# Three GpSimd instructions of a graph-network kernel moved or replaced: a cast, a diagonal select, a running sum

## The chip, the cores and the metric

The kernel runs on one core of one Trainium2 chip. The metric is device time in microseconds (us), the median over runs: 674.09 us before the change (three runs, 673.4 to 678.29). The core has five engines with queues of their own, which meet through semaphores: TensorE (PE, with its weight loads as PEld), VectorE (DVE), ScalarE (ACT), GpSimd (POOL) and SyncE (SP, which here only issues loads).

## What is computed

64 graphs of 128 nodes with 64 features pass through four layers, each followed by a residual sum and a layer norm. The adjacency is symmetric, sparse, and has a 1 on every place of its diagonal (every node has its own loop); the node mask is all ones.

```python
x = _layernorm(x + _L0_gnn_ref(x, adj, ...))            # mean, max, min, std over neighbours
x = _layernorm(x + _L1_gnn_ref(x, adj, weight, bias))   # adj @ (x W) + b
x = _layernorm(x + _L2_gnn_ref(x, adj, nodemask, ...))  # weighted quantiles over a thinned neighbourhood
x = _layernorm(x + _L3_gnn_ref(x, adj))                 # (adj + I) x / row sum
# in L2, the thinning:
adj_ = jnp.where(eye[None], 1.0, adj)                   # every node its own neighbour
nb = (adj_ > 0) & (~eye)[None]
m = nb.sum(-1)
skip = jnp.where(m > 10, (m + 1) // 2, 1)
do_dil = (skip > 1) & mask
removed = nb & do_dil[..., None] & ((rank + 1) % skip[..., None] == 0)
```

## The kernel before

The 64 graphs go in eight turns of eight graphs (`G = 8`, `NG = 8`); `t` is a turn. Work is cut into named steps, and each engine has a hand-written order string (`TENSOR_ORDER`, `SCALAR_ORDER`, `VECTOR_ORDER`, `GPSIMD_ORDER`). An entry `name@lag` means that round `n` issues that step for turn `n + lag`; so one round holds the front of turn n, the middle of turn n-1 and the end of turn n-2. The engines' queues run in order, and a step begins with waits on semaphores. Nothing is scheduled at run time.

What the turn does, with the step names used below:

- `P` (DVE, L1304) makes a permutation matrix per graph, nodes sorted by degree. `Pb` (POOL, step `pb`, L1066) is its bf16 copy, used by the TensorE steps `sm` and `va`. TensorE `yr` (relab<-P,R) and `ap` (relab<-Cc,P) permute the adjacency; ScalarE evicts them in `ysb` (Cc<-relab, L753) and `adj` (adjP, L758).
- `mp` (DVE) makes `maskP`, the permuted 0/1 mask. TensorE `p1` ranks it. Then `se` (POOL, L1070, an affine select over 128x1024 bf16) sets its diagonal to 1 in place, under the name `selfT`. TensorE `va` adds the removed neighbours to it; ScalarE `vt` takes the result as `validT`, from which `p2`, `cr` and ScalarE `sg` make `sgnT`, the signs "has row n more than k neighbours".
- `sk` (POOL, nine instructions over 128x2) works out the skip numbers.
- Layer 0 picks neighbours by one-hot columns (`h0`, TensorE `g0`, evicted by ScalarE `e0` into slot0) and folds them by `tr:0` and `tr:1` (DVE, L1399 and L1413). TensorE `yl:0`/`yl:1` follow, ScalarE scales in `ys:0`/`ys:1` (wv<-pna, L850), DVE adds in `zf:0`/`zf:1` (L1430, L1431). `yl:1` waits for `zf:0`.
- Layer 2 does the same with `h2`, `g2`, `e2` (L908), sorts with a network of 66 min/max instructions (`so`, DVE L1474), weighs (`wr` on TensorE, `wg` on DVE L1487) and sums (`ag`, DVE L1497 and L1501). TensorE `c2:0`/`c2:1` (rest<-x2T,weights) wait for `ag`; between them stands ScalarE's `c2e:0` (hT).
- `n3x` (DVE, L1440) makes the last norm `xo`; `sc` (POOL, L1099) scatters it to HBM in eight indirect DMAs.
- `ov` (POOL, L1092) adds `sgnT` of the turn to a running sum `ovs`. After the last turn `check_counts` (DVE) waits for all of these and tests whether any row had more neighbours than the slots allow; if so, a general path would run (with these inputs it does not).
- `pre` steps are done once, in the first rounds: constants, weights, tables (`tables`, DVE L1208 to L1247; pcol is L1217), and on POOL `split_rows`, five instructions over 128x384 (L1056 to L1060) that split the row factors of turns 2 to 7 in three bf16 parts.

Of the kernel before, what the change touches and what calls it, by code (L numbers as in the profile page):

```python
# [54 lines left out]
KEEP = 4  # L55
# [78 lines left out]
class Turn:  # L134
# [23 lines left out]
    ys:0@0 ysb@1 ys:1@0"""  # L158
# [12 lines left out]
def adj_kernel(nc, x_nat, adj_rows, adj_cols, node_mask, wpack, wrows, out):  # L171

    with ExitStack() as ctx:
# [573 lines left out]
        def scalar_steps(act):  # L747
# [41 lines left out]
            def sg(t):  # L789
# [3 lines left out]
                before(act, "ovs", t, KEEP)  # L793
# [179 lines left out]
            return dict(ysb=ysb, adj=adj, kn=kn, k1=k1, dtc=dtc, vt=vt, k2=k2, sg=sg, xs=xs, qo=qo, pm=pm, pl=pl, rp=rp_, up=up_, ys=ys_, y2e=y2e, z3e=z3e, xr=xr_, xm=xm, xl=xl, ac=ac,  # L973
# [18 lines left out]
        def gpsimd_steps(pool):  # L992
# [123 lines left out]
        def vector_steps(dve):  # L1116
# [86 lines left out]
            def tables():  # L1203
# [28 lines left out]
                for at, to in runs(CAP0):  # L1232
                    V.memset(room0[:, at:to], float(CAP0[at]))
                for at, to in runs(CAP2):
                    V.memset(room2[:, 1 + at:1 + to], float(CAP2[at]))
                V.memset(room2[:, 0:1], 128.0)
                own(V.memset(room2[:, STEPS2 - 1:STEPS2], 0.0))
                V.tensor_tensor(room2[:, :], room2[:, :], step_is[:, :], ALU.mult)
# [515 lines left out]
```

## Time and profile before

| | |
|---|---|
| time, median of 3 runs | 674.09 us |
| span of the profiled execution | 669.3 us |
| PE busy | 491.7 us, 73% |
| DVE busy | 535.6 us, 80% |
| ACT busy | 364.5 us, 54% |
| POOL busy | 144.2 us, 22%, in 211 instructions |
| mean granted TensorE clock | 0.857 of full speed |

The profiled execution's span is 4.8 us under the median. "Busy" counts an instruction from start to end, so it includes the time in which an instruction has started and cannot go on. A row of the timeline reads: start in us, duration in us, engine, line, operation, output<-inputs, shapes, how many merged instructions, and in brackets the idle time before it and what ended that.

### The profile page before, as it was taken

The numbers are of one execution on the slowest core, as the hardware profiler recorded it, in microseconds if no ns is written. First come the engines' busy times: TensorE is split into PE (matmuls) and PEld (weight loads), VectorE is DVE, ScalarE is ACT, GpSimd is POOL, SyncE is SP. The second block draws the span as 40 slices with busy tenths as digits, with TensorE's granted clock in tenths as the row PEclk, the third lists the DMA queues.
The fourth block names the chain that finished last, engine by engine and source line by source line (L and its number), as shares of the span: only waits on it lengthen the run. The fifth ranks groups of instructions, "written<-read, shape, count | busy, mean of one in ns | idle before, by whom it ended". The sixth has DMA issues, their size and how long they took to land.

```text
span 669.3 us, 10465 instructions
## 1 busy us (share of the span) xinstructions
PE 491.7 (73%) x3380; PEld 326.3 (49%) x3419; DVE 535.6 (80%) x1514; ACT 364.5 (54%) x982; POOL 144.2 (22%) x211
## 2 busy tenths in 40 slices
PE   2466968957987889787979898879877986871420
PEld 2432655545655655474547555745564544540220
DVE  4995648998699988999899879997999699469221
ACT  0264577517773678457845685478548852350130
POOL 4500010042004400350035002500251062007023
PEclk9876998979799979999998799889989897555555
DMA  8300020002000200020002000200000000000000
GB/s 315 140 0 0 1 79 1 2 0 80 1 1 11 85 0 1 8 89 1 1 6 90 1 1 6 87 6 1 2 16 1 1 12 5 1 0 16 0 6 14
DMA packets 6573, 18.27 MB, mean 27 GB/s; under 512 B 1648, under 2 KB 1776, under 8 KB 6000
## 3 DMA queue, kind: packets, MB, share of 16 engines
q1 hardware_dynamic: 4464, 15.44, 6.6%
q0 software_dynamic: 2048, 2.10, 1.0%
q8 instruction: 28, 0.46, 0.3%
q14 instruction: 33, 0.27, 0.1%
HBM read 15.44 MB, written 2.10 MB: 26 GB/s over the span
## 4 chain that ended last, share of the span: by engine, by line
DVE 41%; issue 26%; PE 19%; POOL 6%; ACT 6%; POOLq 0%; DVEq 0%; ACTq 0%
DVE hot L1474 8%; DVE slot L1474 8%; DVE slot L1399 6%; PE pna L439 5%; POOL out_dram L1099 4%; PE ring L436 4%; PE pna L436 3%; PE relab L436 2%; PE rest L439 2%; PE rest L436 2%; DVE hot L1487 1%; DVE deg L1143 1%; PE ring L646 1%; DVE hot L1497 1%; DVE slot L1497 1%
## 5 line engine op out<-in xcount | busy, mean ns | idle before, releaser
L436 PE MATMUL ring<-hot,parts 128*64 128x384 bf16 (+3 forms) x753 | 137.9, 361 | 0.9
L1099 POOL DMA_INDIRECT out_dram<-xo,idx x64 | 76.4, 1193 | 130.5 <-DVE xo L1440 112.5
L899 ACT ACTIVATE slot<-ring 128x512 f32<-128x512 f32 (+1 forms) x128 | 61.7, 525 | 38.2 <-PE ring L436 33.9
L850 ACT ACTIVATE wv<-pna,rowP 128x64 f32<-128x64 f32 x128 | 28.0, 330 | 92.6 <-PE pna L436 92.6
L436 PEld LDWEIGHTS ring<-hot,parts 128*128 128x128 bf16 (+1 forms) x768 | 55.6, 108 | 39.9 <-issue 4.3
L1066 POOL CAST Pb<-P 128x1024 bf16<-128x1024 f32 x8 | 8.3, 1038 | 299.6 <-DVE P L1304 299.4
L1399 DVE TENSOR_TENSOR slot<-slot 128x128 f32<-128x128 f32 (+2 forms) x144 | 62.1, 484 | 2.7 <-ACT slot L899 0.7
L439 PE MATMUL ring<-emp,rowsel 112*128 112x512 bf16 (+1 forms) x128 | 45.3, 354 | 13.4 <-ACT slot L899 7.7
L1474 DVE TENSOR_TENSOR hot<-slot 128x64 f32<-128x64 f32 (+5 forms) x136 | 48.8, 392 | 3.8 <-ACT slot L908 3.7
L1474 DVE TENSOR_TENSOR slot<-slot 128x64 f32<-128x64 f32 (+5 forms) x136 | 51.1, 405 | 0.0
L439 PE MATMUL pna<-bdx,xT 128*128 128x384 f32 x64 | 31.5, 579 | 26.5 <-DVE zF L1431 26.5
L439 PE MATMUL rest<-x2T,weights 128*128 128x512 f32 x32 | 24.3, 851 | 23.6 <-DVE x2T L1501 15.9
L908 ACT ACTIVATE slot<-ring 128x384 f32<-128x384 f32 x64 | 31.4, 503 | 16.8 <-PE ring L436 16.4
L436 PE MATMUL pna<-weights,QQ 128*128 128x192 f32 x128 | 37.4, 378 | 0.0
L436 PE MATMUL pna<-wmm,slot 128*128 128x192 f32 x128 | 34.6, 355 | 0.0
L1474 DVE TENSOR_TENSOR hot<-hot 128x128 f32<-128x128 f32 (+3 forms) x96 | 33.4, 375 | 0.0
L1435 DVE TENSOR_REDUCE stB<-sqB 128x8 f32<-128x512 f32 x16 | 10.9, 682 | 26.6 <-ACT sqB L913 26.6
L826 ACT ACTIVATE zB<-rest,rowP 128x64 f32<-128x64 f32 x128 | 28.0, 340 | 6.9 <-PE rest L436 4.0
L1474 DVE TENSOR_TENSOR slot<-hot 128x64 f32<-128x64 f32 (+5 forms) x88 | 31.3, 378 | 0.0
L439 PE MATMUL ring<-sgnT,delta 32*128 32x512 bf16 (+2 forms) x48 | 14.9, 366 | 21.8 <-DVE slot L1487 20.1
L439 PEld LDWEIGHTS ring<-emp,rowsel 112*128 112x128 bf16 x128 | 12.8, 100 | 36.1 <-ACT slot L899 22.9
L439 PE MATMUL pna<-QQ,adjP 128*128 128x128 f32 x128 | 25.4, 379 | 4.8 <-ACT parts L822 4.7
(288 smaller groups left out, 1183.9 us busy)
## 6 DMA issues: line engine op xcount, KB each, us to landing
Cc<-adj_cols_dram SPq DMA_DIRECT2D x8, 512.0 KB, 3.9
R<-adj_rows_dram SPq DMA_DIRECT2D x8, 512.0 KB, 5.4
slot<-adj_rows_dram SPq DMA_DIRECT2D x4, 1024.0 KB, 12.1
xn<-x_nat_dram SPq DMA_DIRECT2D x8, 256.0 KB, 5.5
out_dram<-xo,idx POOLq DMA_INDIRECT x64, 2.3
weights<-wpack_dram SPq DMA_DIRECT2D x1, 608.5 KB, 8.1
biasr<-wrows_dram SPq DMA_DIRECT2D x1, 128.0 KB, 9.0
mask<-node_mask_dram SPq DMA_DIRECT2D x1, 8.0 KB, 4.7
```

The lines of the kernel that those rows point to most:

```text
L436: return mm(*a, start=False, stop=True, skip_group_check=True, **k)
L439: return mm(*a, start=True, stop=True, skip_group_check=True, **k)
L826: last = A(dst[:, g, :], src(g), ACT.Copy, scale=rowP[t.n % ROWKEEP][:, g, which:which + 1])
L850: last = A(ys[:, g, f, :], PQ[:, 256 * g + D * (f + 1):256 * g + D * (f + 2)], ACT.Copy, scale=rowP[t.n % ROWKEEP][:, 4 * h + g, AMP + f:A ...
L899: A(slot0[:, g, lo:hi], PG[ring["g0", t.n, 2 * g + j][0]][:, 0:hi - lo], ACT.Copy).then_inc(s["slot0"], 1)
L908: A(slot2[:, c, lo:hi], PG[ring["g2", t.n, 2 * c + j][0]][:, 0:hi - lo], ACT.Copy).then_inc(s["slot2"], 1)
L1066: V.tensor_copy(flat(Pb[:, :, :]), flat(P[:, :, :])).then_inc(s["Pb"], 1)
L1099: nc.gpsimd.indirect_dma_start(out=out, out_offset=bass.IndirectOffsetOnAxis(ap=idx[t.n % ROWKEEP][:, g:g + 1], axis=0), in_=xo[:, g, :], ...
L1399: return V.tensor_tensor(dst, dst, src, ALU.max)
L1435: V.tensor_reduce(st[:, 0, :], sq[:, :, :], AX.X, ALU.add).then_inc(s[signal], 1)
L1474: mark(("sort", k), V.tensor_tensor(low if is_min else wire(b, 1 - sb_, width), low, high, ALU.min if is_min else ALU.max))
L1497: mark(what, V.tensor_tensor(at, at, ranked(b), ALU.add))
```

## The change

Four things. The cast `pb` leaves POOL and becomes a ScalarE copy, placed between `ys:0` and `ysb`. The select `se` is no longer run in the normal path: `maskP` already has the diagonal when every node has its own loop, so `va` takes it as it is. `ov` and the four wide instructions behind it in `check_counts` go; the room test is left to the layer 0 count alone, whose slots are no wider. To know that the loops are there, a new load brings the diagonals (`own_loop`, 128x64) and a new DVE step `unusual` tests them and the node mask, once, in four instructions.

```diff
-    ys:0@0 ysb@1 ys:1@0"""
+    ys:0@0 pb@1 ysb@1 ys:1@0"""
 ...
     cm@1 so:0-20@-1 z3@-2 so:20-24@-1 n3d@-2 so:24-28@-1 n3x@-2
+    pre:6@-2"""
 GPSIMD_ORDER = """
-    pre:2@0 pre:0@2 sk@0 se@0 pre:1@1 pb@1 sc@-2 ov@-2 pre:3@-1"""
+    pre:2@0 pre:0@2 sk@0 pre:1@1 sc@-2 pre:3@-1"""
 ...
+            sp.dma_start(own_loop[:, :], adj_diag).then_inc(loops_in, 16)
 ...
             def va(t):
                 pe.wait_ge(s["dts"], t.dil())
-                pe.wait_ge(s["selfT"], given(t))
+                if t.fast:
+                    pe.wait_ge(s["maskP"], given(t))
 ...
+            def pb(t):
+                act.wait_ge(s["P"], given(t))
+                before(act, "va_ps", t)
+                A(flat(Pb[:, :, :]), flat(P[:, :, :]), ACT.Copy).then_inc(s["Pb"], 1)
 ...
-            def pb(t):
-                pool.wait_ge(s["P"], given(t))
-                before(pool, "va_ps", t)
-                V.tensor_copy(flat(Pb[:, :, :]), flat(P[:, :, :])).then_inc(s["Pb"], 1)
 ...
-            def ov(t):
-                pool.wait_ge(s["sgnT"], given(t))
-                V.tensor_tensor(flat(ovs[:, :, :]), flat(ovs[:, :, :]), flat(sgnT[t.n % KEEP][:, :, :]),
-                                ALU.add).then_inc(s["ovs"], 1)
 ...
+            def unusual():
+                dve.wait_ge(mask_in, 16)
+                dve.wait_ge(loops_in, 16)
+                dve.wait_ge(rows_in, 2)
+                own(V.tensor_scalar(rtmp[:, 0, :], own_loop[:, :], 0.0, None, ALU.is_le))
+                own(V.tensor_scalar(rtmp[:, 1, :], mask8[:, :], 0.5, None, ALU.is_lt))
+                own(V.tensor_tensor(rtmp[:, 0, :], rtmp[:, 0, :], rtmp[:, 1, :], ALU.max))
+                own(V.tensor_reduce(excess[:, 4:5], rtmp[:, 0, :], AX.X, ALU.max))
 ...
             def check_counts():
-                dve.wait_ge(s["ovs"], NG)
-                dve.wait_ge(s["xo"], NG)
-                own(V.tensor_scalar(tmp, ovs[:, :, :], 0.5 - NG, None, ALU.is_gt))
-                own(V.tensor_scalar(beyond, place[0:32, :], cap2[:, 0:1], None, ALU.is_ge))
-                own(V.tensor_tensor(tmp, tmp, beyond.unsqueeze(1).broadcast_to([32, PAIRS, N]), ALU.mult))
-                own(V.tensor_reduce(excess[0:32, 1:2], tmp.rearrange("p c n -> p (c n)"), AX.X, ALU.max))
-                V.tensor_tensor(excess[:, 3:4], excess[:, 0:1], excess[:, 1:2], ALU.max).then_inc(over_a, 1)
+                V.tensor_tensor(excess[:, 3:4], excess[:, 0:1], excess[:, 4:5], ALU.max).then_inc(over_a, 1)
```

The one-time tables lose the 32-row half of their capacity test (five memsets, a product and a reduction on DVE, one memset on POOL).

GpSimd's queue, around the second and third rounds. Before, the select, the cast for the next turn and the five `split_rows` instructions stand behind one another (L1086 is the last of the nine `sk` instructions):

```order
L1086 TENSOR_TENSOR skp<-skp 128x2
L1070 AFFINE_SELECT maskP<-maskP 128x1024
L1066 CAST Pb<-P 128x1024
L1056 CAST rowsb<-rows 128x48x8
L1057 TENSOR_TENSOR xo<-rows,rowsb 128x48x8
L1058 CAST rowsb<-xo 128x48x8
L1059 TENSOR_TENSOR xo<-xo,rowsb 128x48x8
L1060 CAST rowsb<-xo 128x48x8
L1078 TENSOR_SCALAR skp<-dcol 128x2
```

The same place in the changed kernel (its lines are numbered some 12 higher):

```order
L1093 TENSOR_TENSOR skp<-skp 128x2
L1068 CAST rowsb<-rows 128x48x8
L1069 TENSOR_TENSOR xo<-rows,rowsb 128x48x8
L1070 CAST rowsb<-xo 128x48x8
L1071 TENSOR_TENSOR xo<-xo,rowsb 128x48x8
L1072 CAST rowsb<-xo 128x48x8
L1085 TENSOR_SCALAR skp<-dcol 128x2
```

The five split instructions no longer stand behind the cast, which waits for the next turn's P; they follow `sk` and wait for the row factors alone.

ScalarE's queue, where round n-1 ends its layer 0 scaling (`ys:0` and `ys:1`). Before:

```order
L899 ACTIVATE slot<-ring 128x328
L850 ACTIVATE wv<-pna,rowP 128x64 x8
L753 ACTIVATE Cc<-relab 128x1024
L850 ACTIVATE wv<-pna,rowP 128x64 x8
L758 ACTIVATE adjP<-relab 128x1024
```

In the changed kernel:

```order
L912 ACTIVATE slot<-ring 128x328
L863 ACTIVATE wv<-pna,rowP 128x64 x8
L772 ACTIVATE Pb<-P 128x1024
L762 ACTIVATE Cc<-relab 128x1024
L863 ACTIVATE wv<-pna,rowP 128x64 x8
L767 ACTIVATE adjP<-relab 128x1024
```

The cast stands ahead of the eviction `ysb`, so `ysb` waits for it too. The same holds at the program's start, where the cast of turn 0 is the third instruction of the queue and `ysb` of turn 0 the fourth.

## Rows read from the trace of the kernel before

**Rows 1.** Timeline of POOL, the cast Pb in three rounds (start, duration, ...)

```profile
276.80 1.04 POOL L1066 CAST Pb<-P 128x1024 bf16<-128x1024 f32 x1 [44.92 <-DVE P L1304]
343.77 1.04 POOL L1066 CAST Pb<-P 128x1024 bf16<-128x1024 f32 x1 [43.04 <-DVE P L1304]
412.96 1.04 POOL L1066 CAST Pb<-P 128x1024 bf16<-128x1024 f32 x1 [45.26 <-DVE P L1304]
```

**Rows 2.** Chain that ended last, one round: start, us, what

```profile
343.70 2.78 DVE slot L1399 x6
...
356.87 1.11 DVE slot L1474
...
366.67 1.12 DVE hot L1497
```

**Rows 3.** POOL's groups by line and shape: busy us, mean ns | idle before

```profile
L1092 POOL TENSOR_TENSOR ovs<-ovs,sgnT 32x512 bf16<-32x512 bf16 x8 | 11.9, 1486 | 0.2
L1070 POOL TENSOR_SCALAR_AFFINE_SELECT maskP<-maskP 128x1024 bf16<-128x1024 bf16 x8 | 10.6, 1325 | 12.8 <-PE relab L439 12.8
L1066 POOL CAST Pb<-P 128x1024 bf16<-128x1024 f32 x8 | 8.3, 1038 | 299.6 <-DVE P L1304 299.4 <-POOL rowsb L1060 0.2
```

**Rows 4.** Timeline of DVE: the same instructions with and without POOL beside them

```profile
151.47 0.22 DVE L1474 TENSOR_TENSOR slot<-slot,hot 128x64 f32<-128x64 f32 x1
...
336.23 2.47 DVE L1399 TENSOR_TENSOR slot<-slot 128x128 f32<-128x128 f32 x7
...
343.62 3.31 DVE L1399 TENSOR_TENSOR slot<-slot 128x128 f32<-128x128 f32 x7
...
356.79 1.17 DVE L1474 TENSOR_TENSOR slot<-slot,hot 128x64 f32<-128x64 f32 x1
...
567.59 0.22 DVE L1497 TENSOR_TENSOR hot<-hot,slot 128x64 f32<-128x64 f32 x1
```

**Rows 5.** Timeline of ACT and DVE around ysb, ys:1 and zf:1 of one round

```profile
212.00 1.02 ACT L753 ACTIVATE Cc<-relab 128x1024 f32<-128x1024 f32 x1 [0.76 <-PE relab L439]
221.20 1.75 ACT L850 ACTIVATE wv<-pna,rowP 128x64 f32<-128x64 f32 x8 [8.17 <-PE pna L436]
223.37 0.42 DVE L1430 TENSOR_TENSOR zF<-pna,wv 128x256 f32<-128x256 f32 x1
```

**Rows 6.** Timeline of DVE around the five split_rows instructions

```profile
116.91 0.22 DVE L1474 TENSOR_TENSOR hot<-slot 128x64 f32<-128x64 f32 x1 [1.32 <-ACT slot L908]
...
134.60 5.58 DVE L1399 TENSOR_TENSOR slot<-slot 128x128 f32<-128x128 f32 x7
```

**Rows 7.** A ScalarE group, SBUF to SBUF; one small DVE instruction in a chain of its kind

```profile
L966 ACT ACTIVATE parts<-rest_ 128x512 bf16<-128x512 f32 x8 | 5.0, 631 | 4.1 <-DVE rest_ L1526 4.1
...
112.16 0.19 DVE L1149 TENSOR_SCALAR rows<-rows 128x48 f32<-128x48 f32 x1
```

**Rows 8.** The start: a piece of the chain that ended last

```profile
16.61 0.92 ACT Cc L753
```

**Rows 9.** The end: timeline, and the landing of the scatters (last number, us)

```profile
656.75 0.96 POOL L1099 DMA_INDIRECT out_dram<-xo,idx  x1 [0.30 <-issue]
658.99 0.41 DVE L1631 TENSOR_SCALAR zB<-ovs 32x512 f32<-32x512 bf16 x1 [11.13 <-POOL ovs L1092]
...
662.10 0.14 DVE L1638 CAST overi<-over 1x1 int32<-1x1 f32 x1
...
out_dram<-xo,idx POOLq DMA_INDIRECT x64, 2.3
```

**Rows 10.** Timeline of PE: matmuls behind waits, in two rounds

```profile
305.54 1.10 PE L439 MATMUL rest<-x2T,weights 128*128 128x512 f32 x2 [0.98 <-ACT hT L971]
...
350.95 0.88 PE L439 MATMUL pna<-bdx,xT 128*128 128x384 f32 x2 [3.16 <-DVE zF L1431]
...
370.41 1.13 PE L439 MATMUL rest<-x2T,weights 128*128 128x512 f32 x2 [1.83 <-DVE x2T L1501]
...
372.51 2.05 PE L439 MATMUL rest<-x2T,weights 128*128 128x512 f32 x2 [0.98 <-ACT hT L971]
```

More of the change, by code:

```diff
@@ L41 @@
 W0, W2 = sum(CAP0), sum(CAP2)
+assert CAP2 == CAP0[:K2] and K0 == K2 + 2 and DILATE_ABOVE == K2 - 1
 SPLIT0, SPLIT2 = OFF0[4], OFF2[3]
@@ L163, with adj_kernel @@
     h2:6-8@-1 h0:3-4@0 h2:8-11@-1 h0:4-9@0 me@0 ng@0 we@0 z2@-2 n2d@-2 h0:9-13@0 n2x@-2 pre:5@-1 em@0 pre:4@0
-    cm@1 so:0-20@-1 z3@-2 so:20-24@-1 n3d@-2 so:24-28@-1 n3x@-2"""
+    cm@1 so:0-20@-1 z3@-2 so:20-24@-1 n3d@-2 so:24-28@-1 n3x@-2
+    pre:6@-2"""
 GPSIMD_ORDER = """
-    pre:2@0 pre:0@2 sk@0 se@0 pre:1@1 pb@1 sc@-2 ov@-2 pre:3@-1"""
+    pre:2@0 pre:0@2 sk@0 pre:1@1 sc@-2 pre:3@-1"""
 SYNC_ORDER = """
     lc@-1 lr@-1 lx@-1"""
-def adj_kernel(nc, x_nat, adj_rows, adj_cols, node_mask, wpack, wrows, out):
+def adj_kernel(nc, x_nat, adj_rows, adj_cols, adj_diag, node_mask, wpack, wrows, out):
     with ExitStack() as ctx:
@@ L330, in adj_kernel @@
         mask_in = sem("mask_in")
+        loops_in = sem("loops_in")
         bias_in = sem("bias_in")
@@ L347, in given, with late @@
             return t.n * per + (per if k is None else k)
+        def late(t, per=1, k=None):
+            return t.g * per + (per if k is None else k)
         def before(eng, name, t, back=1, per=1, k=None):
@@ L511, in va @@
                 pe.wait_ge(s["dts"], t.dil())
-                pe.wait_ge(s["selfT"], given(t))
+                if t.fast:
+                    pe.wait_ge(s["maskP"], given(t))
+                else:
+                    pe.wait_ge(s["selfT"], late(t))
                 for h in range(2):
@@ L792, in sg @@
                 before(act, "g2_ps", t, KEEP, 2 * PAIRS)
-                before(act, "ovs", t, KEEP)
                 if not t.fast:
@@ L971, in c2e @@
                 A(hT[:, a, :, :].rearrange("p c n -> p (c n)"), PZ[:, 512:1024], ACT.Relu, bias=b1t).then_inc(s["hT"], 1)
-            return dict(ysb=ysb, adj=adj, kn=kn, k1=k1, dtc=dtc, vt=vt, k2=k2, sg=sg, xs=xs, qo=qo, pm=pm, pl=pl, rp=rp_, up=up_, ys=ys_, y2e=y2e, z3e=z3e, xr=xr_, xm=xm, xl=xl, ac=ac,
+            return dict(ysb=ysb, pb=pb, adj=adj, kn=kn, k1=k1, dtc=dtc, vt=vt, k2=k2, sg=sg, xs=xs, qo=qo, pm=pm, pl=pl, rp=rp_, up=up_, ys=ys_, y2e=y2e, z3e=z3e, xr=xr_, xm=xm, xl=xl, ac=ac,
                         sd=sd, mts=mts, e0=e0, e2=e2, n0q=n0q, n0r=n0r, n1q=n1q, n1r=n1r, n2q=n2q, n2r=n2r, n3q=n3q,
@@ L1232, in tables @@
                 for at, to in runs(CAP0):
[L1233 to L1238, printed above, removed]
+                    mark("own", V.memset(room0[:, at:to], float(CAP0[at])))
+                need("own")
                 own(V.tensor_tensor(room0[:, :], room0[:, :], slot_is[:, :], ALU.mult))
                 V.tensor_reduce(cap0[:, :], room0[:, :], AX.X, ALU.add)
-                V.tensor_reduce(cap2[:, :], room2[:, :], AX.X, ALU.add)
                 step2 = step_is[:, 1:1 + K2].unsqueeze(2).broadcast_to([32, K2, D])
@@ L1638, in check_counts @@
                 V.tensor_copy(overi[0:1, :], over[0:1, :]).then_inc(over_c, 1)
-            once = (prepare, weigh_in, tables, rank_weights, lambda: degrees(OTHERS), lambda: factors(OTHERS, 2))
+            once = (prepare, weigh_in, tables, rank_weights, lambda: degrees(OTHERS), lambda: factors(OTHERS, 2),
+                    unusual)
             def pre(t, k):
@@ L1666, in adj_kernel @@
                 b1 b2 b3 general2 c2:0 c2:1 c3 c6""",
-            "scalar": """ysb adj kn:0 k1 dtc:0 kn:1 dtc:1 kn:2 dtc:2 kn:3 dtc:3 vt k2 sg xs qo pm pl rp up ac sd mts
+            "scalar": """pb ysb adj kn:0 k1 dtc:0 kn:1 dtc:1 kn:2 dtc:2 kn:3 dtc:3 vt k2 sg xs qo pm pl rp up ac sd mts
                 ys:0 ys:1 n0q n0r b1e n1q n1r b3e xh xm xl c2e:0 c2e:1 y2e n2q n2r xr z3e n3q n3r""",
-            "gpsimd": "pb sk:0 se sk:1 sk:2 sk:3 sc",
+            "gpsimd": "sk:0 se sk:1 sk:2 sk:3 sc",
             "vector": """cm gt P nb:0 mp rw dr:0 nb:1 dr:1 nb:2 dr:2 nb:3 dr:3 ng me we general0 zf:0 zf:1
```

16 lines of the change are left out of this document (5 added, 11 removed).

## The prediction

> **What bounds the kernel now.** The page comes first: DVE is the busiest engine (80%), PE next (73%), and POOL is busy for 22% only, so GpSimd is not short of time. What matters is whom it stops. The chain that ended last, read for one round, answers that. A round is what lies between two casts Pb: 343.77 - 276.80 = 66.97 us, and 412.96 - 343.77 = 69.19 us [rows 1]. In each the chain runs on DVE through the sort, the folds and the weighing to the sum `ag`, then over PE's and ACT's steps from `c2:0` to the last `g2`, and back to DVE's sort. In DVE's part stand three pieces that are longer than their neighbours: the folds at 343.70, one sort instruction at 356.87 and one instruction of `ag` at 366.67 [rows 2].
>
> The timeline of DVE says why. The same seven folds take 2.47 us in `tr:0` and 3.31 us in `tr:1`, which runs while POOL casts Pb at 343.77 [rows 1, 4]: 0.84 us lost. A sort instruction over 128x64 takes 0.22 us in the round that has no `ov`, and 1.17 us in the round that has one [rows 4]: 0.95 us lost. An instruction of `ag` takes 0.22 us where no `se` runs [rows 4] and 1.12 us where one does [rows 2]: 0.90 us lost. Together 2.69 us of a round of 67 to 69 us, all of them on the chain; POOL's three instructions last 1.04, 1.49 and 1.33 us on average [rows 3].
>
> A rule of the Trainium skill speaks to this: "SBUF — State Buffer" says that VectorE and GpSimd share a pair of SBUF ports under an exclusive lock, held for a whole instruction, and that a VectorE instruction with two SBUF inputs contends with a GpSimd instruction that reads SBUF. Read strictly, the rule would have DVE lose each POOL instruction's whole length, an estimate of 3.9 us a round by their means, and the three removals together could give 6 x 1.04 + 6 x 1.33 + 7 x 1.49 = 24.7 us. The trace agrees on who is stopped, but shows 2.69 us a round, 17.1 us over the same counts; the sum goes by the rows.
>
> **The change part by part.** Rounds with a cast and a sort in full swing: casts of turns 2 to 7, six of them (in turn 1, near 74 us, DVE waits for ACT anyway, and I count nothing). Selects of turns 2 to 7, six; that of turn 1 falls into a wait of DVE.
>
> *Cast off POOL:* 6 x 0.84 = 5.0 us. On ACT the copy of 128x1024 has no row. From below it costs 0.63 us, the 128x512 copy between SBUF tiles, from above twice that, 1.26 [rows 7]; I take 1.05. It is hidden: before `ysb` ACT idles 0.76 us, so `ysb` slips by 0.3 (by 0.5 at the upper bound), and behind it ACT idles another 8.17 us before `ys:1` [rows 5]. What waits for `ysb` (`ap` on PE, `nb` on DVE) is queued behind `yl:1` and `zf:1`, some 9 us later; what waits for `Pb` (`sm`) is later still. Without that cover it would cost 1.05 a round.
>
> *Select removed:* 6 x 0.90 = 5.4 us. It lies just ahead of `c2:0`, which waits for `ag`, and nothing else holds `c2:0`.
>
> *Running sum removed:* seven lie in the rounds or the drain, each 0.95 on DVE. But the next meeting point is `zf:1`: `ys:1` ends at 221.20 + 1.75 = 222.95 and `zf:1` starts at 223.37 [rows 5], so DVE had 0.42 us to spare over ACT. DVE, freed of 0.95, arrives early and waits. I count 7 x 0.4 = 2.8; between 0 and 6.6.
>
> *split_rows moves:* beside it and the cast the folds took 5.58 instead of 2.47 us [rows 4, 6]. Its five instructions now start as soon as DVE has made the row factors, which is just ahead of a place where DVE waits 1.32 us for ACT and then sorts [rows 6]. Only what falls into the wait is free: between 0 and 1.3, I take 0.7.
>
> *Start:* DVE carries nearly all of the chain there too. The select of turn 0 ran beside the table pcol; I take 0.9, as in the rounds. The cast of turn 0 no longer stalls DVE (0.8), but on ACT it pushes `ysb` of turn 0, which is on the chain [rows 8], back by about 1.0. The tables' dropped small instructions give 0.3, of which little passes, since ACT's results are due soon after. Net 0.9, between -0.3 and 2.
>
> *unusual:* four chained instructions on DVE in the round that ends turn 0, at 0.19 us [rows 7] and a hand-over each: costs 0.9 us, on the chain. Its inputs have been there for long. The load behind it, 32 KB once, stands last in SP's first batch, and the loads of turn 1 queued behind it wait for turn 0's data to be used anyway: 0.
>
> *Scatters:* no longer behind the cast, they start some 10 us earlier in a round, beside `tr:0`. A scatter is not on the chain, and `n3x` waits for the one before for a whole round. 0.
>
> *End:* the last scatter is issued at 656.75 and lands about 2.3 us later, at 659.05. Now the test's last instruction ends at 662.10 + 0.14 = 662.24, because it waits for `ov`, which stands behind eight scatters (11.13 us of waiting) [rows 9]. After the change the test is done long before, and the landing sets the end: 3.2 us.
>
> Sum: 5.0 + 5.4 + 2.8 + 0.7 + 0.9 - 0.9 + 3.2 = 17.1 us.
>
> *The clock.* PE's granted clock falls to the lower level (1.2 of 2.4 GHz) at two places of a round. Behind its wait of 3.16 us for `zf:0` [rows 10] it fell in all five rounds from 208 us on. Around `c2:1` it fell in some rounds only: the same two matmuls take 2.05 us in one and 1.10 in the other [rows 10], and the round with the fall is 69.19 - 66.97 = 2.2 us longer [rows 1]. The granted clock by stretches shows such a fall in four of six rounds, at most 4 x 2.2 = 8.8 us in all. What PE did before it: little, with a wait of 1.83 us for `ag` in it [rows 10]. This wait shrinks by the select's 0.90, and the 3.16 by the cast's 0.84. So falls should get rarer, not more frequent. I take 3 us, a third of the 8.8; the bounds are -2 and +10 (the latter with the first place cured too, which lets `ov`'s other 0.55 a round through).
>
> Total 20.1 us. Against the profiled execution's span: 669.3 - 20.1 = 649.2 us. That span lies 4.8 under the median, and I carry that over: 674.1 - 20.1 = **654.0 us**.
>
> **The rivals.**
> - *Half of it is absorbed.* DVE's freed time turns into waits for ACT and PE, as shown for `ov`. For it: PE is busy 73%, and `zf:1` has 0.42 us of slack only. Against it: the cast's and the select's losses stand directly ahead of `zf:0` and `c2:0`, for which PE waits 3.16 and 1.83 us. With `ov` at 0, the clock as before and the cast or the select at half: 17.1 - 2.8 - 2.7 = 11.6, so 662; down to 8 us, 666. Chance 0.22.
> - *The clock stays up.* 17.1 + 8 to 10 us: 647 to 649. For it: the round that kept it at `c2:1` had the same waits, so it was close already. Against it: 2.3 us of idling before `yl:1` remain. Chance 0.15.
> - *The stalls stay.* DVE's long instructions come from something else that stays, the scatters say, or ScalarE's copy now stops DVE. Then only the end's 3.2 us and little more come: 670, within 1%. Against it: the stalls sit on different lines and go with POOL's instruction each time, and ACT copies between SBUF tiles all along. Chance 0.04.
> - *Slower.* The copy on ACT is slow or waits late, and `ys:1` slips. It decides from where the copy passes the cover: 0.76 + 8.17 = 8.9 us. To end over 1% slower it must lose 17 + 6.7 us in seven rounds, 3.4 each beyond the cover: a copy of 12.3 us, ten times the upper bound. Chance 0.02.
> - The forecast itself, a gain of 15 to 24 us, 650 to 659: 0.57.
>
> **How the numbers follow.** The predicted time is the forecast's. The range takes the forecast, nearly all of the clock case, and the better half of the absorbed case: 646 to 662. About 1% of the time, 6.7 us, is what a measurement can tell from no change. Faster by more: 0.57 + 0.15 + 0.21 of the absorbed case = 0.93; within 1%: 0.05; slower 0.02.
>
> **What would show it.** In the profile after: no L1399 group of seven above 2.5 us outside the split; the 128x64 instructions of the sort and of `ag` at 0.22 throughout; POOL busy down by some 30 us; ACT's Pb copy near 1.05 us, and idle behind it; a wait of about 0.5 us of DVE at `zf:1` for ACT; PE's wait before `yl:1` at 2.3 and before `c2:0` at 0.9; rounds of 64 to 66.5 us; the last DVE instruction ahead of the last scatter. Long folds beside a scatter would prove the stall theory wrong; short folds with rounds as long as before would prove the chain wrong.

## The result, and the profile after

The changed kernel takes 649.19 us (median of four runs, 646.34 to 652.76) against 673.75 us (median of four) for the kernel before in the same comparison: a ratio of 0.9676, 95% interval 0.9636 to 0.9716, or 24.6 us less. The forecast was 654.0, its range 646 to 662. The profiled execution took 646.34 us with a span of 644.8, that of before had 669.3: 24.5 us.

The head of the page after (spans in us):

```profile
span 644.8 us, 10421 instructions
...
PE 482.3 (75%) x3380; PEld 320.0 (50%) x3419; DVE 514.6 (80%) x1504; ACT 370.4 (57%) x990; POOL 112.8 (17%) x186
...
PEclk9866998999899989989998999899989997555555
```

POOL's busy time falls by 31.4 us, DVE's by 21.0. The mean granted clock is 0.874 against 0.857. The timeline of DVE, at the folds of one `tr:1` and at the `zf:1` of the next round, shows what [rows 1, 4] showed of before, now without POOL beside it, and a new wait:

```profile
266.76 2.46 DVE L1404 TENSOR_TENSOR slot<-slot 128x128 f32<-128x128 f32 x7
...
343.94 0.22 DVE L1479 TENSOR_TENSOR slot<-slot,hot 128x64 f32<-128x64 f32 x1
...
345.98 0.42 DVE L1435 TENSOR_TENSOR zF<-pna,wv 128x256 f32<-128x256 f32 x1 [0.49 <-ACT wv L863]
```

The seven folds take 2.46 us where they took 3.31, the 128x64 instruction of the sort 0.22 where it took 1.17, and DVE waits 0.49 us for ScalarE at `zf:1`, as forecast. ScalarE in the same round (timeline):

```profile
334.92 1.10 ACT L772 ACTIVATE Pb<-P 128x1024 bf16<-128x1024 f32 x1
335.86 1.07 ACT L762 ACTIVATE Cc<-relab 128x1024 f32<-128x1024 f32 x1
344.19 1.75 ACT L863 ACTIVATE wv<-pna,rowP 128x64 f32<-128x64 f32 x8 [7.26 <-PE pna L442]
```

The cast takes 1.10 us there (1.04 to 1.11 over the eight), `ysb` stands behind it, and 7.26 us of idling are left ahead of `ys:1` [rows 5: 8.17].

Rounds, cut at the start of P, first of before and then of after. Behind the length of a round stand the busy time (and number of instructions) of PE, PEld, DVE, ACT and POOL, then the granted clock, the DMA share and GB/s:

```profile
206.66:275.51 68.85, 58.31 (x424) 39.08 (x428) 61.82 (x171) 44.61 (x122) 15.31 (x20) 0.93 0.08 24
275.51:342.48 66.97, 55.81 (x424) 37.11 (x428) 61.73 (x172) 44.28 (x122) 15.32 (x20) 0.97 0.08 25
342.48:411.67 69.19, 58.65 (x424) 39.55 (x428) 61.83 (x171) 44.60 (x122) 15.31 (x20) 0.93 0.07 24
411.67:480.11 68.44, 57.40 (x424) 38.77 (x428) 61.81 (x172) 44.50 (x122) 15.33 (x20) 0.95 0.07 24
```

```profile
199.70:265.62 65.92, 56.01 (x424) 37.69 (x428) 59.15 (x172) 45.34 (x123) 10.46 (x17) 0.97 0.08 25
265.62:330.50 64.88, 55.87 (x424) 37.52 (x428) 59.17 (x171) 45.07 (x123) 11.91 (x18) 0.97 0.08 25
330.50:395.39 64.89, 55.89 (x424) 37.52 (x428) 59.17 (x171) 45.06 (x123) 11.92 (x18) 0.97 0.08 26
395.39:460.27 64.88, 55.89 (x424) 37.53 (x428) 59.17 (x171) 45.07 (x123) 11.91 (x18) 0.97 0.08 25
```

Two of these compare like with like: the rounds with the clock at 0.97 that fall only behind `zf:0`, 66.97 before and 64.88 after. They differ by 2.09 us. The sum had 0.84 + 0.90 + 0.4 = 2.14. The other three rounds of before are 1.5 to 2.2 us longer at a clock of 0.93 to 0.95; after the change one round is 1.0 longer, and none falls under 0.97.

Where the 24.5 us lie, by the same marks in both traces:

| stretch | before | after | won | in the sum |
|---|---|---|---|---|
| start to P of turn 1 | 72.95 | 70.17 | 2.78 | 0.9 |
| to P of turn 3 | 133.71 | 129.53 | 4.18 | 0.84 + 0.90 + 0.7 - 0.9 = 1.54 |
| to P of turn 7 (four rounds) | 273.45 | 260.57 | 12.88 | 4 x 2.14 = 8.56, and clock |
| to the last xo | 166.79 | 162.87 | 3.92 | 0.84 + 0.90 + 3 x 0.4 = 2.94 |
| last xo to the end | 22.4 | 21.6 | 0.8 | 3.2 |
| total | 669.3 | 644.8 | 24.5 | 17.1, and 3 for the clock |

### The profile page after: what moved, and what is told of

Read it like the earlier page. It is cut to its first block, busy times and chain, and to the rows that moved or that the text cites. A ratio compares the mean times of both kernels' runs of the same rounds, so it can differ in the third digit from the quotient of the medians.

```text
span 644.8 us, 10421 instructions
## 1 busy us (share of the span) xinstructions
PE 482.3 (75%) x3380; PEld 320.0 (50%) x3419; DVE 514.6 (80%) x1504; ACT 370.4 (57%) x990; POOL 112.8 (17%) x186
## 4 chain that ended last, share of the span: by engine, by line
DVE 34%; issue 27%; PE 22%; ACT 8%; POOL 6%; POOLq 0%; DVEq 0%; ACTq 0%
DVE hot L1479 7%; DVE slot L1479 7%; PE pna L445 6%; DVE slot L1404 5%; PE pna L442 5%; POOL out_dram L1099 5%; PE ring L442 4%; PE relab L442 2%; PE rest L442 2%; DVE deg L1143 1%; ACT wv L863 1%; PE ring L655 1%; DVE slot L1502 1%; DVE P L1309 1%; DVE hot L1492 1%
## 5 line engine op out<-in xcount | busy, mean ns | idle before, releaser
L1099 POOL DMA_INDIRECT out_dram<-xo,idx x64 | 78.1, 1220 | 309.9 <-DVE xo L1445 292.9
L1404 DVE TENSOR_TENSOR slot<-slot 128x128 f32<-128x128 f32 (+2 forms) x144 | 53.1, 424 | 2.8 <-ACT slot L912 0.9
L1479 DVE TENSOR_TENSOR hot<-slot 128x64 f32<-128x64 f32 (+5 forms) x136 | 50.8, 407 | 3.5 <-ACT slot L921 3.5
L445 PE MATMUL pna<-bdx,xT 128*128 128x384 f32 x64 | 28.6, 530 | 16.5 <-DVE zF L1436 16.5
L445 PE MATMUL rest<-x2T,weights 128*128 128x512 f32 x32 | 22.3, 785 | 18.1 <-DVE x2T L1506 10.4
L1085 POOL TENSOR_SCALAR skp<-dcol 128x2 f32<-128x2 f32 x8 | 2.1, 264 | 175.7 <-ACT dcol L780 175.7
L445 PE MATMUL ring<-sgnT,delta 32*128 32x512 bf16 (+2 forms) x48 | 14.6, 364 | 22.4 <-DVE slot L1492 20.3
L839 ACT ACTIVATE m<-pna,rowP 128x64 f32<-128x64 f32 x128 | 28.7, 394 | 0.1
```

The costliest lines, as they stand in the source:

```text
L445: return mm(*a, start=True, stop=True, skip_group_check=True, **k)
L839: last = A(dst[:, g, :], src(g), ACT.Copy, scale=rowP[t.n % ROWKEEP][:, g, which:which + 1])
L1099: nc.gpsimd.indirect_dma_start(out=out, out_offset=bass.IndirectOffsetOnAxis(ap=idx[t.n % ROWKEEP][:, g:g + 1], axis=0), in_=xo[:, g, :], ...
L1404: return V.tensor_tensor(dst, dst, src, ALU.max)
L1479: mark(("sort", k), V.tensor_tensor(low if is_min else wire(b, 1 - sb_, width), low, high, ALU.min if is_min else ALU.max))
```

## The experiments

### One part alone

Three kernels each take one part of the change to the kernel before.

```diff
 # the cast alone
-    ys:0@0 ysb@1 ys:1@0
+    ys:0@0 pb@1 ysb@1 ys:1@0
-    ... sk@0 se@0 pre:1@1 pb@1 sc@-2 ov@-2 ...
+    ... sk@0 se@0 pre:1@1 sc@-2 ov@-2 ...
```

> The kernel before with the cast alone moved to ScalarE. Stall theory: the seven folds beside the cast fall from 3.31 to 2.47 us in six rounds, 5.0 us, less 0.2 at the start (0.8 won on DVE, 1.0 lost on ysb of turn 0), plus 0.7 for the split: 5.5 us, 668 against 674. PE's wait for zf:0 falls from 3.16 to about 2.3, TensorE's clock falls behind it still. Absorbed theory: the 0.84 us turns into a wait for ACT at zf:1, so less than 2 us are won. Clock theory (the gain of the whole change is mostly fewer falls of the clock around c2:1): no gain of that kind here, since the wait for ag stays 1.83.

Measured: 666.18 us against 670.46, ratio 0.9949 (0.9917 to 0.9982), some 3.4 us. The profiled span was 663.6.

```diff
 # the select alone
-    ... sk@0 se@0 pre:1@1 ...
+    ... sk@0 pre:1@1 ...
+                if t.fast:
+                    pe.wait_ge(s["maskP"], given(t))
```

> The kernel before with the select alone left out, va waits for maskP. Stall theory: instructions of ag all at 0.22 us, 6 x 0.90 = 5.4, plus 0.9 at the start: 6.3 us. Clock theory: PE's wait for ag falls from 1.83 to 0.93, and with it the fall of the granted clock around c2:1 goes in most of the four rounds that show it, up to 8.8 us on top: 6 to 15 us, and the second c2 matmul pair takes 1.10 in each round. Absorbed theory: under 3 us.

Measured: four runs, 652.76, 664.87, 665.84 and 671.43 us, against 670.46. Their mean granted clocks were 0.892, 0.861, 0.854 and 0.844, in the same order: the same program, and 18.7 us between the runs. No ratio is given for them: by their median the select alone is worth 5.1 us, by the fastest run 17.7. The rounds say more. In the profiled execution one round (337.08 to 403.12) has a clock of 0.97 and its one fall behind `zf:0`, as the like round of before has; it takes 66.04 us against 66.97, which is 0.93 less where the sum had 0.90.

```diff
 # the running sum alone
-    ... sc@-2 ov@-2 ...
+    ... sc@-2 ...
-                own(V.tensor_scalar(tmp, ovs[:, :, :], 0.5 - NG, None, ALU.is_gt))
 ...
```

> The kernel before with the running sum and its test alone left out. As predicted: 0.4 us in each of seven rounds, 2.8, and 3.2 at the end: 6.0. As the changed kernel's trace suggests: the end gives 0.7 only, because something behind the last scatter holds the end 11.8 us from its issue, so 2.8 + 0.7 = 3.5 us, and DVE waits about 0.5 us for ScalarE at zf:1. With ov's 0.95 let through in full where the clock stays up: up to 6 us in the rounds.

Measured: 669.29 us, ratio 0.9997 (0.9967 to 1.0027): nothing.

The stalls first. The groups of DVE's 128x64 instructions in the sort and in `ag`, with mean ns behind the comma, first of the kernel with the sum alone removed:

```profile
L1473 DVE TENSOR_TENSOR slot<-slot,hot 128x64 f32<-128x64 f32 x40 | 8.6, 214 | 0.0
L1496 DVE TENSOR_TENSOR hot<-hot,slot 128x64 f32<-128x64 f32 x8 | 7.1, 888 | 0.0
```

and of the kernel with the select alone removed:

```profile
L1480 DVE TENSOR_TENSOR slot<-slot,hot 128x64 f32<-128x64 f32 x40 | 13.4, 334 | 0.0
L1503 DVE TENSOR_TENSOR hot<-hot,slot 128x64 f32<-128x64 f32 x8 | 1.7, 216 | 0.0
```

With the sum gone the sort is at 214 ns and `ag` still at 888; with the select gone `ag` is at 216 and the sort still at 334. So the sum's and the select's stalls were assigned rightly. DVE's busy time in the four rounds from P of turn 3 to P of turn 7 adds up too: a round has 0.73 us less without the cast, 0.95 less without the select and 0.88 less without the sum, 2.56 together, against 2.63 in the changed kernel.

But the times do not follow. With the cast alone gone, the seven folds of `tr:1` take 2.46 us in every round, and yet the four rounds (200.94 to 474.64) take 273.70 us, no less than before. The trace of that kernel shows why. GpSimd's queue no longer waits for P, so the scatters run earlier, and with them the running sum moves: it now stands beside the last two folds, ahead of `zf:0` (POOL and DVE):

```profile
273.50 1.39 POOL L1092 TENSOR_TENSOR ovs<-ovs,sgnT 32x512 bf16<-32x512 bf16 x1
```

```profile
273.80 1.91 DVE L1399 TENSOR_TENSOR slot<-slot 128x128 f32<-128x128 f32 x2
```

These two folds take 0.94 us in the kernel before:

```profile
347.45 0.94 DVE L1399 TENSOR_TENSOR slot<-slot 128x128 f32<-128x128 f32 x2
```

So ahead of `zf:0` DVE wins 0.85 us and loses 0.97, and PE's wait for `zf:0` goes from 3.16 to 3.28 us. What DVE wins behind `zf:0`, where the sum no longer stands, becomes a wait at `zf:1`:

```profile
355.95 0.42 DVE L1430 TENSOR_TENSOR zF<-pna,wv 128x256 f32<-128x256 f32 x1 [1.91 <-ACT wv L855]
```

That wait is for `ys:1`, behind a `yl:1` that ran wholly at the lower clock; in a round where the clock recovered sooner the wait is 0.30. "The cast alone" is therefore not the cast's stall alone: the kernel puts another stall in its place. The 5.7 us by which its profiled execution is shorter lie at the start (1.6) and in the two rounds where `split_rows` moved (4.1). In the full change this cannot happen, since the sum is gone as well.

With the sum alone gone, PE's second `c2` pair took 2.03 to 2.05 us in all six rounds from 167 us on, against 1.94 to 2.05 in three of six in the kernel before (the others 1.10), so what DVE gave back, the clock took.

### The cast put back, and two probes in its place

These start from the changed kernel.

```diff
-    ys:0@0 pb@1 ysb@1 ys:1@0
+    ys:0@0 ysb@1 ys:1@0
-    ... pre:1@1 sc@-2 ...
+    ... pre:1@1 pb@1 sc@-2 ...
```

> The changed kernel with the cast alone put back on GpSimd, in its old place between the split and the scatters. Stall theory: folds of tr:1 at 3.3 again in six rounds, 5.0 us slower than the changed kernel, and 0.8 at the start against 1.0 won on ysb; 654 to 655 against 649. If the wait for zf:0 grows back to about 3.2 and brings falls of the clock in the rounds that had none: up to 2 us more. Absorbed theory: DVE has 0.5 us to spare at zf:1 now, so only 0.35 of the 0.84 us a round is lost, 2 us.

Measured: 653.49 us, ratio 0.9745 (0.9701 to 0.9788), span 651.8: 4.3 us over the changed kernel by the medians. The folds of `tr:1` are back at 3.31 us. That is just under the expected 654 to 655.

The next two leave the real cast on ScalarE and give GpSimd something without use in its old place:

```diff
+            def pz(t):
+                pool.wait_ge(s["P"], given(t))
 ...
+                V.tensor_copy(scratch[:, 0:1024], flat(P[:, :, :]))   # e5
+                V.memset(scratch[:, 0:1200], 0.0)                     # e6, in its stead
 ...
-    ... pre:1@1 sc@-2 ...
+    ... pre:1@1 pz@1 sc@-2 ...
```

> The changed kernel plus one GpSimd cast a turn from P into a tile that nobody reads, in the old cast's place (128x1024 f32 to bf16, 1.04 us). Stall theory (GpSimd's port use stops the folds): the folds of tr:1 take 3.3 instead of 2.46 us in each round, some 5 us slower than the changed kernel: 650 to 655 of span, as in the run with the cast put back. Dependency theory (the old cast cost time because Pb came late or because of its semaphores): nothing waits for this one, so the folds stay at 2.46 and the time at the changed kernel's.

> The same with a memset of 128x1200 bf16, which writes SBUF for about as long (1.05 us by biasb's 1.81 us for 2048) and reads nothing. If what stops VectorE is GpSimd's reading, the folds stay at 2.46 and the span within 1 us of the changed kernel's with the same clock. If any use of SBUF by GpSimd stops it, the folds take 3.3 again and the run is like that with the cast.

Measured: with the read 656.17 us, ratio 0.969 (0.957 to 0.981), span 654.5; with the write 650.29, ratio 0.964 (0.955 to 0.973), span 649.4. The intervals overlap; the rows decide. Timelines of POOL and DVE, with the cast without use:

```profile
270.16 1.04 POOL L1080 CAST scratch<-P 128x1024 bf16<-128x1024 f32 x1 [46.02 <-DVE P L1317]
```

```profile
270.01 3.31 DVE L1412 TENSOR_TENSOR slot<-slot 128x128 f32<-128x128 f32 x7
```

and with the memset:

```profile
269.88 1.10 POOL L1080 MEMSET scratch<- 128x1200 bf16 x1 [45.18 <-DVE P L1317]
```

```profile
269.74 2.46 DVE L1412 TENSOR_TENSOR slot<-slot 128x128 f32<-128x128 f32 x7
```

A cast that nobody waits for costs the folds the same 0.85 us as the real one. A memset that is slightly longer and writes the same SBUF costs them nothing. So for the cast it is GpSimd's reading that stops VectorE, not a late Pb, a semaphore, or SBUF traffic as such. That is also what the Trainium skill, "SBUF — State Buffer" (Who interferes with whom), states: a VectorE instruction with two SBUF inputs contends with a GpSimd instruction that reads SBUF, not with one that only writes. The traces agree on that. The page says further (SBUF: two separate sides) that the one which starts first has the ports for its whole instruction and the other is blocked. The traces show a little less, 0.85 us lost of 1.04, and don't show where the rest is. The select and the sum were only removed, not replaced by such a pair of probes. GpSimd's scatters lie beside `tr:0` and `tr:1` in the changed kernel, and the folds take 2.47 and 2.46 us there, as without them.

Both probes also queue the second `split_rows` behind their instruction, as the kernel before did. With the memset, P of turn 1 to P of turn 3 takes 131.31 us (71.63 to 202.94), in the changed kernel 129.53 (70.17 to 199.70). PE's wait for `zf:0` in there is 6.08 us in place of 1.07. By this pair the split's new place is worth up to 1.8 us; other kernels with the split in its new place took 129.6 to 131.3, so the clock can take most of that again.

### Filling PE's wait

```diff
+            def fz(t):
 ...
+                pe.wait_ge(s["x2"], t.n)
 ...
+                for k in range(9):      # 12 in the kernel before
+                    new(bank(PZ, 0), identb[:, :], onesb[:, :])
-    ... yr@0 yl:1@-1
+    ... yr@0 fz@-1 yl:1@-1
```

> The changed kernel plus nine matmuls of 512 columns without use in PE's wait of 2.33 us for zf:0, seven times. Clock theory: the granted clock no longer falls behind this wait, yl:1 runs at 0.81 and 0.49 throughout, DVE's wait of 0.5 us at zf:1 goes, and a round takes 64.2 instead of 64.9 us in the four rounds that had the fall: 3 us faster, span 642. Rival: a round that kept its clock at the first place tends to lose it around c2:1 instead (as 199.7 to 265.6 in the changed kernel did, 65.8 to 65.9 us), so the fill moves the fall and the time stays or grows by up to 1 us a round. Slower by 0.2 a round if the nine do not fit into the wait.

> The kernel before plus twelve matmuls of 512 columns without use in PE's wait of 3.16 us for zf:0, seven times. It holds the clock at the first place in both kernels, so that what is left between this run and the filled changed kernel (span 642.0) is what the change itself takes off the chain. Stall theory: rounds of 66.5 us (64.3 of the filled changed kernel plus 0.84 + 0.90 + 0.4), span near 660, 18 us above the filled changed kernel. Clock theory (the change's gain is mostly clock): the span comes within 10 us of 642. If the fall around c2:1 stays, since its wait of 1.83 us for ag is untouched, rounds stay at 68 to 69 and the span at 665 to 669.

Measured on the changed kernel: 646.0 us, ratio 0.9588 (0.9501 to 0.9675), four spans from 642.0 to 644.6. The rounds of the profiled execution:

```profile
202.13:266.41 64.28, 56.88 (x438) 36.89 (x437) 59.02 (x171) 45.11 (x123) 10.46 (x17) 1.00 0.08 25
266.41:330.69 64.28, 56.88 (x438) 36.87 (x437) 59.03 (x171) 45.11 (x123) 11.88 (x18) 1.00 0.09 26
330.69:394.96 64.27, 56.88 (x438) 36.87 (x437) 59.02 (x172) 45.12 (x123) 11.89 (x18) 1.00 0.08 26
394.96:460.78 65.82, 58.44 (x438) 38.45 (x437) 59.11 (x171) 45.33 (x123) 11.88 (x18) 0.97 0.08 25
```

Three rounds keep the full clock, DVE's wait at `zf:1` is gone, and they take 64.28 us, 0.6 less than the 64.88 with a fall. This is the 0.5 us of `ov` that the forecast had only in its upper bound. In the kernel before the same kind of edit gives nothing: 670.17 us, ratio 0.9976 (0.9935 to 1.0018), though the mean clock of its ten runs was 0.859 to 0.875, against 0.844 to 0.863 without the fill. Two rounds of its profiled execution, which at 676.29 us is 6 us longer than the median:

```profile
205.57:275.58 70.01, 60.47 (x435) 39.40 (x440) 61.68 (x171) 44.65 (x122) 15.43 (x20) 0.93 0.07 24
275.58:346.92 71.34, 61.86 (x435) 40.62 (x440) 61.88 (x172) 44.84 (x122) 15.25 (x20) 0.90 0.07 23
```

The first two matmuls of `yl:1` took 0.88 us, as at full clock, in every round from 205 us on. The fall came a few microseconds later instead (PE's timeline; `xt` took 1.09 us in the kernel before at full clock):

```profile
284.05 0.88 PE L439 MATMUL pna<-bdx,xT 128*128 128x384 f32 x2 [0.57 <-DVE zF L1439]
...
293.31 1.97 PE L439 MATMUL pna<-P,xn 128*64 128x128 f32 x16 [0.36 <-DVE zF L1439]
...
306.06 1.82 PE L439 MATMUL rest<-x2T,weights 128*128 128x512 f32 x2 [2.40 <-DVE x2T L1509]
308.87 2.05 PE L439 MATMUL rest<-x2T,weights 128*128 128x512 f32 x2 [0.98 <-ACT hT L979]
```

So curing the clock at one place can move its fall to another, and in the kernel before it did. Filled kernel against filled kernel the change is worth 24.2 us by the medians (670.17 - 646.0). The stall theory expected 18 and the clock theory less than 10, and neither came out. Nearest came the third case of that expectation, that the fall around `c2:1` stays and the span is 665 to 669: the ten spans run from 666.1 to 675.8, with a median of 668.3, but the rounds of the profiled execution grew to as much as 71.3 us, which it did not foresee. What PE must have done for the clock to fall just there is left open.

### The end

```diff
 # behind the last turn's eight scatters (e8)
+                if t.n == NG - 1:
 ...
+                    own(V.tensor_tensor(flat(ovs[:, :, :]), flat(ovs[:, :, :]), flat(sgnT[t.n % KEEP][:, :, :]), ALU.add))
 # or in their stead, on SP (e10)
+            sp.wait_ge(s["xo"], NG)
+            sp.dma_start(last, xo[:, :, :]).then_inc(last_out, 16)
 ...
```

The second of these leaves out the last turn's scatters, so its last 1024 rows lie in sorted order and not in their places; it serves this question alone. Each has one run: 650.4 and 637.43 us.

> The changed kernel plus one GpSimd instruction behind the last scatter (the running sum's 32x512 addition, some 1.2 us when alone). In the changed kernel 11.83 us lie between the start of the last scatter and the end. If the end hangs on GpSimd's queue running dry, they grow by 1.2 to 13.0. If it hangs on the landing of the last scatter and its signal, they stay 11.8.

> The changed kernel, but the last turn's 1024 rows are stored by one plain load-queue transfer of SP in their sorted order, without its eight scatters; these rows are not put in their places. GpSimd's last instruction is then a scatter of the turn before. If the end hangs on GpSimd's queue running dry, nothing of GpSimd is late any more, and the end comes about 7 us behind the test's last instruction (625.08 + 0.14 + 7.06 = 632.3), or about 4 us (the median landing of such transfers) plus a few behind the last xo at 623.1: 631 to 634. If it hangs on a fixed time behind the last store of any kind, 623.2 + 11.8 = 635.

From the start of the last scatter to the end it is 12.6 us in the kernel before, 11.8 in the changed one, 11.4 with the sum alone removed, and 12.8 with the instruction put behind the scatters. That is the growth that the queue case of the expectation gives. The view of the line at which the program's engines meet for the last time shows what these are made of. `POOLq` is GpSimd's sequencer. Each engine runs a DRAIN there, and GpSimd's EVENT_SEMAPHORE, which comes behind the last of them, lets all go on to read the test's result. A row has durations in ns, then the start; start and duration give the end, so GpSimd's DRAIN ends at 647.7 + 16.5 = 664.2. Before:

```profile
L1656 POOLq EVENT_SEMAPHORE  x2: 17/17/17, 664.3 to 664.3; - x2
...
L1656 POOLq DRAIN  x1: 16490/16490/16490, 647.7 to 647.7; - x1
...
L1656 DVEq DRAIN  x1: 180/180/180, 662.1 to 662.1; - x1
```

After:

```profile
L1654 POOLq EVENT_SEMAPHORE  x2: 17/17/17, 639.3 to 639.4; - x2
...
L1654 POOLq DRAIN  x1: 15337/15337/15337, 623.9 to 623.9; - x1
...
L1654 SPq COMPARE_BRANCH  x1: 33/33/33, 635.1 to 635.1; - x1
```

And without the last scatters:

```profile
L1661 POOLq EVENT_SEMAPHORE  x2: 17/17/17, 630.5 to 630.6; - x2
L1661 POOLq DRAIN  x1: 17677/17677/17677, 584.2 to 584.2; - x1
...
L1661 DVEq DRAIN  x1: 178/178/178, 628.9 to 628.9; - x1
L1661 SPq COMPARE_BRANCH  x1: 33/33/33, 630.4 to 630.4; - x1
```

SP's COMPARE_BRANCH stands behind SP's wait for the scatters, so in the changed kernel they had all landed by 635.1, about as the forecast had it (2.2 us behind the start of the last). But GpSimd's DRAIN went on to 639.2, which is 5.3 us behind its last instruction (633.9). In the kernel before it is the same 5.3 us (658.9 to 664.2), and so it is, 5.29 to 5.33 us, in every kernel of this study in which the last turn is scattered (with the added instruction, from GpSimd's wait behind it). VectorE's DRAIN was over at 662.3 there, 1.9 us sooner. So the test did not set the end in the kernel before either; GpSimd did. Without the last scatters GpSimd is done at 601.9, and SP's wait for its plain store, until 630.3, comes last. The end, 635.8, is 6.8 us behind the test (629.0), as one case of the expectation had it, but it is the store that holds it. The other case, a fixed 11.8 us behind the last store's start, is out: the last `xo` came at 626.96 here, and the end would have been near 639.

Behind the meeting come 0.8 to 0.9 us in all kernels, and then one branch of PE, which is the last thing in the trace:

```profile
bacc.py:44 PEldq COMPARE_BRANCH  x1: 4238/4238/4238, 665.1 to 665.1; - x1
```

This is of the kernel before; it takes 4.66 us in the changed one, 4.2 to 4.7 in all kernels without filling matmuls and 3.3 to 3.6 in the four with them. Why it differs is open. The end's gain adds up from these rows: 1.2 us for the running sum ahead of the DRAIN, less 0.4 for that branch, 0.8. Against a plain store the last eight scatters cost 12.8 us: 21.6 us from the last `xo` to the end in the changed kernel, 8.8 without them (626.96 to 635.8).

### A better version

```diff
-    ys:0@0 pb@1 ysb@1 ys:1@0
+    ys:0@0 ysb@1 pb@1 ys:1@0
-    pre:6@-2"""
+"""
             def check_counts():
+                unusual()
 # and the nine filling matmuls ahead of yl:1
```

> The changed kernel with three edits: the nine filling matmuls, the cast of a turn behind ysb instead of ahead of it, and the loop and mask test at the end of the program, ahead of the count test, where the scatters cover it. Against the filled changed kernel (span 642.0 to 644.6): 1.0 us less at the start, since ysb of turn 0 no longer waits for the cast, and 0.98 less in the round that ends turn 0: 640 to 642.6. If the end hung on VectorE's test it would give 0.8 back, and if Pb came too late for sm, PE would wait for ScalarE there.

Measured: 642.47 us, ratio 0.9591 (0.9551 to 0.963), four spans from 637.7 to 641.8, that of the profiled run 639.2. P of turn 1 starts at 69.61 us (70.88 in the filled kernel), and the loop test costs nothing that shows behind the last `xo`: 20.5 us to the end, 20.3 in the filled kernel. By its interval the gain over the filled kernel isn't shown; by the spans (642.0 to 644.6 there) it is about 3 us.

```diff
+            def fd(t, n):               # last turn alone
+                if t.n == NG - 1:
+                    pe.wait_ge(s["xT2"], given(t))
+                    for k in range(n):
+                        new(bank(PZ, 0), identb[:, :], onesb[:, :])
 # fd:36 ahead of wr:2, fd:10 ahead of c2:0, fd:4 ahead of c2:1, fd:10 ahead of c6
```

> The same plus 60 filling matmuls in PE's waits of the last turn (36 ahead of wr:2, ten ahead of c2:0, four ahead of c2:1, ten ahead of c6), where the granted clock is at the lower level from 550 us on. If the clock comes back, c2:0 and c2:1 take 1.1 instead of 2.05 each, the hidden sum c3 about 1.9 instead of 3.5, c6 1.9 instead of 3.7: 5 us less. If it stays low in spite of them, the ten matmuls ahead of c2:0 take 4.3 us of a wait of 4.7 and the four take 1.7 of 1.0: 1 us more.

Measured: 634.98 us, ratio 0.9466 (0.9436 to 0.9496), four spans from 629.9 to 637.8. It is the fastest of the study, 14 us under the changed kernel. PE's timeline of the profiled run, the slowest of the four:

```profile
597.08 1.50 PE L444 MATMUL rest<-x2T,weights 128*128 128x512 f32 x2 [0.36 <-DVE x2T L1519]
...
599.56 1.10 PE L444 MATMUL rest<-x2T,weights 128*128 128x512 f32 x2
...
601.66 1.90 PE L441 MATMUL rest<-weights,hT 128*128 128x64 f32 x16
...
608.95 3.68 PE L444 MATMUL rest<-x,adjP 128*128 128x64 f32 x16 [3.23 <-DVE x L1458]
```

`c2:1` and `c3` run at the full clock (1.10 and 1.90 us; 2.05 and 3.51 after the change), `c6` does not yet, since PE waited 3.23 us behind the ten matmuls ahead of it.

## Why the prediction was right, and where not

- **The stalls.** Right, in mechanism and size. The like rounds differ by 2.09 us against 2.14 in the sum, the select alone gives 0.93 in a like round against 0.90, and the cast put back costs 4.3 us against 5.0 for its term. The rival "the stalls stay" is refuted by the folds and the 128x64 instructions after the change.
- **The cast on ScalarE.** 1.10 us against the 1.05 taken, `ysb` slips, and `ys:1` still has 7.26 us of idling ahead of it. The rival "slower" had no ground.
- **The running sum.** The 0.4 us a round was right where the clock falls behind `zf:0` (the wait of 0.49 at `zf:1` is the rest of the 0.95). Where it does not fall the whole 0.95 passes. Alone, on the kernel before, it gave nothing; the prediction had that as the low end of the term (between 0 and 6.6) and in its absorbed case, though there for DVE's waits and not for the clock.
- **The end.** The step that failed: "the landing sets the end: 3.2 us" measured 0.8. The landing itself was read rightly, but it doesn't set the end, and VectorE's test didn't set it before. The forecast took the 7.06 us behind the test's last instruction as what follows the test. In the traces GpSimd's DRAIN, 5.3 us behind its last instruction, comes later than the test in the kernel before (664.2 against 662.3) and later than the landing in the changed one (639.2 against 635.1). The change took off only the running sum's 1.2 us ahead of that DRAIN.
- **The start.** Under-sized: 2.78 against 0.9. Up to P of turn 1 the cast alone won 1.6 us where the forecast had -0.2, the select alone 1.8 where it had 0.9, the sum alone 0.3. The cast on ScalarE did push `ysb` of turn 0 back, by 0.94 us; putting the cast behind `ysb` brought P of turn 1 from 70.88 to 69.61 us in the filled kernels. Which stalls of the start made up the rest is open.
- **The split.** 0.7 was taken. DVE itself won about that: the folds beside it fell by 3.1 us and the two behind them by 1.5, of which the cast had 0.84, but the sort's first instructions now run beside the split and lose 3.0. The prediction's step stopped there; PE's wait of 6.90 us for `zf:0` in that round went to 1.07, and the granted clock of the round that follows P of turn 2 is 0.97 where it was 0.91.
- **The clock.** 3 us were taken. By the rounds it is 4.5 in the four middle ones (three rounds of before are 1.5 to 2.2 longer than 66.97, 5.6 in all, one of after is 1.0 longer), and the 2.6 us more than summed between P of turn 1 and P of turn 3 belong to it in part. The direction was read rightly from the waits ahead of `c2:0` and `yl:1`: the first went from 1.83 to 0.93, and the second `c2` pair took 1.10 us in five of six rounds instead of three; the second wait from 3.16 to 2.33, and there the fall stayed.

So the total is 4.4 us better than the forecast because the clock and the start gave more than was taken, while the end gave 2.4 less. That the sum came close is in part errors that cancel, the end against the start. The kernels with one part each can't be added up against the whole. The cast alone gave about 3.4 us where the stall theory expected 5.5, since the sum moved into its place; the sum alone gave nothing where 3.5 to 6.0 were expected; the select alone gave 5 us by its median and 17.7 by its fastest run. Whether three removals are worth more together than apart is therefore open in the times, while DVE's busy time adds up to 0.07 us a round.

## What to carry to other kernels

Look at GpSimd by whom it stops, not by how busy it is: compare one VectorE instruction with two SBUF inputs with and without a GpSimd instruction that reads SBUF beside it, and price the removal by that difference and not by GpSimd's duration; a memset there is free. Where one instruction is taken from GpSimd's queue, look at what moves up behind it: here a running sum came to stand beside folds ahead of `zf:0` and cost there about what the cast had cost (0.97 us against 0.85). Where TensorE idles between short bursts, compare only rounds at the same granted clock. Before counting a gain at the end of a program, look at what each engine's sequencer still does there, and which one is last.

## What the runs showed of the hardware

- GpSimd's write-only memset of 1.10 us cost the folds beside it nothing, a cast of 1.04 us cost them 0.85.
- GpSimd can lose time as well. In the kernel before, the running sum takes 1.17 us with no VectorE work beside it (657.73) and 1.49 us in the rounds, where it costs VectorE 0.95. The cast takes 1.04 us each time.
- With the last turn scattered, GpSimd's last DRAIN ended 5.29 to 5.33 us behind the instruction or wait ahead of it in all thirteen kernels.
- One program's runs differed by 18.7 us with the mean granted clock (652.76 us at 0.892, 671.43 at 0.844): more than three times the 5.4 us that its edit had in the sum.
- PE kept the lower clock through a stretch with matmuls almost without pause. In the last kernel, whose PE is busy for all of the 10 us of the first row, the clock is 0.50 there, and 0.71 in the third, where the filling matmuls begin (577.10) (granted clock by stretches):

```profile
555.00:565.00 10.00, 10.00 (x75) 4.29 (x71) 1.65 (x4) 5.27 (x16) 0.00 (x0) 0.50 0.00 0
565.00:575.00 10.00, 7.63 (x40) 5.16 (x36) 8.00 (x26) 5.29 (x19) 0.00 (x0) 0.50 0.01 2
575.00:585.00 10.00, 7.90 (x29) 3.37 (x31) 9.97 (x35) 0.78 (x2) 5.60 (x5) 0.71 0.04 13
```
